# Window attention and a mixture of experts on one core: token repeats by DMA alone on two queues, the output sum on ScalarE and GpSimd, the selectors of the first norm later

## What is computed

```python
x = x + conv(_ln_c(x))        # norm over channels, then the attention layer
t = tokens(x)                 # 4096 tokens of 32 channels an image
t = t + ffn(_ln_t(t))         # norm over channels, then 8 experts, the best 2
# conv: instance norm over the picture with weight and bias; qkv = 1x1 conv;
#   windows of 8x8, 4 heads of 8 channels; softmax(q k / sqrt(8)) v; 1x1 projection
# ffn:  probs = softmax(x @ router_w + router_b); top 2, rescaled to sum 1;
#   y = sum over the two experts of p * (x @ expert_w[e] + expert_b[e])
```

## Time and profile before

| | us |
|---|---|
| runs | 397.84, 402.92, 404.67 |
| median | 402.92 |
| profiled execution | 405.62 |
| its span, first to last instruction | 403.6 |
| first scores (L596) start | 47.3 |
| last turn into the experts, about | 290 |

### The profile page before, as it was taken

One profiled execution on the slowest core, in us unless ns is written; L12 is line 12 of the kernel. 1 busy time (PEld: TensorE's weight loads), 2 busy tenths in 40 slices (PEclk: granted clock), 3 DMA queues, 4 the chain that ended last, 5 costly groups with the idle time before them and its releaser, 6 DMA issues.

```text
span 403.6 us, 12568 instructions
## 1 busy us (share of the span) xinstructions
PE 360.6 (89%) x5318; PEld 189.1 (47%) x5318; DVE 335.2 (83%) x435; ACT 260.5 (65%) x448; POOL 162.4 (40%) x191
## 2 busy tenths in 40 slices
PE   5979689999999999999999999998898897778985
PEld 2545446665665655566566656565421221111220
DVE  1477968988988979998998979999967999996785
ACT  3735557777787798678788797775464664423331
POOL 8600000111202202378634102478593558438543
PEclk9988969999999999999999999999998999896999
DMA  8600000031000000000000100022314543533541
GB/s 306 286 2 4 2 0 3 2 74 35 4 2 4 2 3 2 2 3 2 3 2 22 37 2 3 2 59 69 87 39 107 144 123 106 139 112 96 149 139 52
DMA packets 12870, 22.49 MB, mean 56 GB/s; under 512 B 2960, under 2 KB 5136, under 8 KB 12432
## 3 DMA queue, kind: packets, MB, share of 16 engines
q1 hardware_dynamic: 12240, 19.93, 17.1%
q10 hardware_dynamic: 576, 1.77, 1.1%
HBM read 5.96 MB, written 4.19 MB: 25 GB/s over the span
## 4 chain that ended last, share of the span: by engine, by line
PE 57%; DVE 24%; ACT 7%; issue 5%; DMA 4%; POOL 2%; ACTq 0%; POOLq 0%; DVEq 0%
PE psum L609 13%; PE psum L626 8%; PE psum L596 6%; PE psum L634 4%; PE psum L571 4%; DMA gate_f<-gate_sel 4%; PE psum L760 3%; PE psum L566 3%; PE psum L444 3%; DVE probs L1292 3%; DVE neg_max L1149 3%; DVE window_work L1152 2%; PE psum L772 2%; PE psum L580 2%; DVE probs L1289 2%
## 5 line engine op out<-in xcount | busy, mean ns | idle before, releaser
L327 POOL TENSOR_TENSOR o_norm<-o_tok,o_rden 128x128 f32<-128x128 f32 x64 | 25.4, 418 | 178.7 <-DVE o_rden L1162 178.7
L609 PE MATMUL psum<-weights_sb,window_work 128*128 128x128 f32 x512 | 82.1, 283 | 7.0 <-DVE window_work L1152 4.0
L894 ACT ACTIVATE probs<-psum 128x512 f32<-128x512 f32 x128 | 74.8, 595 | 17.5 <-PE psum L609 15.2
L609 PEld LDWEIGHTS psum<-weights_sb,window_work 128*128 128x128 f32 x512 | 57.9, 141 | 49.6 <-issue 28.8
L1152 DVE TENSOR_TENSOR window_work<-psum,neg_max 128x1024 f32<-128x1024 f32 x64 | 78.4, 1225 | 2.2
L1149 DVE TENSOR_REDUCE neg_max<-psum 128x16 f32<-128x1024 f32 x64 | 76.8, 1199 | 4.0 <-PE psum L596 4.0
L626 PE MATMUL psum<-probs,v_cols 128*32 128x64 f32 x2048 | 54.8, 225 | 0.3 <-DVE o_tok L1160 0.2
L626 PEld LDWEIGHTS psum<-probs,v_cols 128*32 128x32 f32 x2048 | 34.8, 109 | 28.2 <-issue 24.8
L878 ACT ACTIVATE stage<-k_sb,weights_sb 128x512 f32<-128x512 f32 x64 | 44.1, 719 | 0.0
L1160 DVE STREAM_TRANSPOSE o_tok<-psum 128x512 f32<-128x512 f32 x32 | 22.9, 716 | 21.1 <-PE psum L626 21.1
L596 PE MATMUL psum<-stage 32*64 32x256 f32 x1024 | 35.8, 387 | 1.9 <-DVE proj_bias L1136 1.0
(11 more groups left out here) (131 smaller groups left out, 612.4 us busy)
## 6 DMA issues: line engine op xcount, KB each, us to landing
stage<-act_all SPq DMA_DIRECT2D x144, 64.0 KB, 2.0
out<-out_sb SPq DMA_DIRECT2D x16, 256.0 KB, 2.0
stage<-in_x SPq DMA_DIRECT2D x3, 1024.0 KB, 12.4
gate_rows<-gate_parts SPq DMA_DIRECT2D x16, 128.0 KB, 2.6
weights_sb<-weights ACTq DMA_DIRECT2D x1, 811.5 KB, 11.7
stage<-in_x SPq DMA_DIRECT2D x1, 768.0 KB, 5.3
gate_f<-gate_sel ACTq DMA_DIRECT2D x1, 512.0 KB, 14.9
weights_sb<-weights ACTq DMA_DIRECT2D x1, 320.0 KB, 7.7
```

Source lines behind the costliest of these rows:

```text
L327: last = pool.tensor_tensor(o_norm[:, hf, :, p * 16:p * 16 + 16].rearrange("p g (b d) -> p g b d", b=2), t[:, p * 8:p * 8 + 8, :].rearrang ...
L609: last = nc.tensor.transpose(bank[TURN_BANKS[v % 2]][:, b * P:b * P + P], heads.rearrange("p h k -> p (h k)"), const["c_ident"][:, :])
L894: nc.scalar.activation(probs[:, w % 4, :], bank[TURN_BANKS[w % 2]][:, :], ACT.Exp).then_inc(exp_done, 1)
```

## The change

1. All four images of all chunks are repeated by DMA, two chunks in one (32 partitions by 4 KB). Slots hold a pair of chunks and there are three: `stage[:, 0:4096]`, `stage[:, 4096:8192]` and `x_win[:, 0:4096]`, which was the work space of the gates of quads 0 and 1. Pairs 0 and 1 are issued by SP alone; from pair 2 on SP issues images 2 and 3 and ScalarE's queue images 0 and 1, eight DMAs each. `replicate`, `keep_tokens` and `centre_rep` are gone. The queries move to `out_sb`.
2. The sum of a chunk: ScalarE copies the PSUM bank to `y_sb` (in the space of `v_cols`), GpSimd adds `act_all`. Only the last chunk is summed by VectorE. `bias` waits for the copy instead of the sum.
3. Gate step 21 of quads 2 and 3 moves from VectorE to GpSimd, and steps 22 and 23 stand together before the scaling of a half.
4. In the first norm the selector table is loaded ahead of the last piece of the weights, `regroup` is made first, and `sel_sum` between quads 0 and 1. `instance_deviation(1)` stands behind the forming of chunk 1's input, and TensorE waits for `biases_ready` only at the second turn of chunk 0.

```diff
-SPLITS, SLOTS = 3, 4
+SPLITS, SLOTS = 3, 3
...
-        q_two = stage[:, 0:2 * CHUNK].rearrange("p (u n) -> p u n", u=2)
-        x_rep = stage[:, :].rearrange("p (s b n) -> p s b n", s=SLOTS, b=IMG)
+        x_reps = [t.rearrange("p (b u n) -> p b u n", b=IMG, u=2)
+                  for t in (stage[:, 0:half], stage[:, half:2 * half], x_win[:, 0:half])]
+        q_two = out_sb
+        y_sb = v_flat[:, 0:2 * CHUNK].rearrange("p (u n) -> p u n", u=2)
...
+        def wait_tokens(engine, c):
+            pair = c // 2
+            k, turns = pair % SLOTS, pair // SLOTS
+            engine.wait_ge(reps_in[k], 16 * ((16 if k < REP_FIRST else 8) + 8 * turns))
+            by_act = 8 * turns + (0 if k < REP_FIRST else 8)
+            if by_act > 0:
+                engine.wait_ge(reps_by_act[k], 16 * by_act)
+        def repeat_pair(engine, pair, images, done):
+            at = slice(pair * 2 * CHUNK, (pair + 1) * 2 * CHUNK)
+            for b in images:
+                for e in range(4):
+                    engine.dma_start(x_reps[pair % SLOTS][C * e:C * e + C, b, :, :],
+                                     act_all[C * b:C * b + C, at].rearrange("p (u n) -> p u n", u=2)
+                                     ).then_inc(done[pair % SLOTS], 16)
+        def wait_slot(engine, pair):
+            if pair >= SLOTS:
+                engine.wait_ge(y_step, (pair - SLOTS) * 4 + 4)
+            elif pair == 2:
+                engine.wait_ge(gate_step[1], GATE_OPS + ONE)
+            elif pair == 1:
+                engine.wait_ge(score_ps, CHUNKS * 2)
...
-            for h, n in ((1, 6), (4, 14), (6, 22), (7, 23), (8, 26), (8, 27), (9, 29)):
+            for h, n in ((1, 6), (4, 14), (6, 21), (7, 22), (7, 23), (8, 26), (8, 27), (9, 29)):
...
# SP
+            def repeat_tokens(pair):
+                sp.wait_ge(x2_done, min(pair * 2 + 2, CHUNKS) + X2)
+                wait_slot(sp, pair)
+                repeat_pair(sp, pair, range(0 if pair < REP_FIRST else 2, IMG), reps_in)
...
             for c in range(CHUNKS):
-                if c + 3 < CHUNKS:
-                    repeat_tokens(c + 3)
                 if c % QUAD == 2 and c // QUAD + 1 < QUADS:
                     move_gates(c // QUAD + 1)
+                if c == 2:
+                    repeat_tokens(2)
+                if c >= 2 and c % 2 == 0 and c // 2 + 2 < CHUNKS // 2:
+                    repeat_tokens(c // 2 + 2)
...
# GpSimd, after scale(c, eh)
+                    if eh == 1 and c >= 1:
+                        combine(c - 1)
...
# TensorE
+                if n == 0 and v == 1:
+                    pe.wait_ge(biases_ready, 1)
...
-            pe.wait_ge(biases_ready, 1)
+            pe.wait_ge(ln1["normed"], CHUNKS + NORMED)
             chunk(0, 0, first=True)
...
-                wait_past(pe, summed, c - 1)
+                wait_past(pe, y_kept, c - 1)
...
# ScalarE
+            act.dma_start(gate_in, io["gate_sel"]).then_inc(gate_in_loaded, 16)
             act.dma_start(weights[:, second_cols:], io["weights"][:, second_cols:]).then_inc(weights_loaded, 16)
-            act.dma_start(gate_in, io["gate_sel"]).then_inc(gate_in_loaded, 16)
...
+                    if first and hf == 0:
+                        instance_deviation(1)
...
+            def keep_sum(c):
+                act.wait_ge(y_step, c * 2 + 2)
+                wait_past(act, summed, c - 1)
+                nc.scalar.activation(y_sb[:, c % 2, :], bank[6 + c % 2][:, :], ACT.Copy).then_inc(y_kept, 1)
...
                     copy_gates(c, eh)
+                    if eh == 1 and c >= 1:
+                        keep_sum(c - 1)
...
-                    if eh == 0 and c + REP_FIRST < CHUNKS:
-                        keep_tokens(c + REP_FIRST, 0)
+                    if (c, eh) == (2, 1):
+                        repeat_tokens(2)
+                    if eh == 0 and c >= 3 and c % 2 == 1 and (c + 3) // 2 < CHUNKS // 2:
+                        repeat_tokens((c + 3) // 2)
...
# VectorE
-            selectors()
+            regroups()
             for quad in range(QUADS):
+                if quad == 1:
+                    selectors()
                 first_norm(quad)
...
-            HALF_STEPS = ((0, 1, 2), (3, 4, 5), (7, 8), (9, 10, 11, 12), (13,), (15, 16), (17, 18, 19, 20, 21), (24,))
+            HALF_STEPS = ((0, 1, 2), (3, 4, 5), (7, 8), (9, 10, 11, 12), (13,), (15, 16), (17, 18, 19, 20), (24,))
...
-                    if eh == 0 and c >= 1:
-                        combine(c - 1)
```

More of the change, by code:

```diff
@@ L182, in metaformer_block @@
         reps_in = [sem(f"reps_in{k}") for k in range(SLOTS)]
-        rep_ps = sem("rep_ps")
-        rep_done = sem("rep_done")
+        reps_by_act = [sem(f"reps_by_act{k}") for k in range(SLOTS)]
         raw_done = sem("raw_done")
@@ L430, in _ @@
                     for quad, n in late:
-                        if n != 23:
+                        if n not in (22, 23):
                             gates(quad, n)
@@ L732, in _ @@
                 chunk(m, m % 2, final=(m == CHUNKS - 1))
-            def replicate(c, first_bank):
-                for b in range(2):
-                    rows = slice(32 * b, 32 * b + 32)
-                    last = nc.tensor.matmul(bank[first_bank + b][:, :], centre_rep[rows, :],
-                                            act_all[rows, c * CHUNK:c * CHUNK + CHUNK], start=True, stop=True)
-                last.then_inc(rep_ps, 1)
             def gate_pair(c, eh, pair):
@@ L1008, in copy_gates, with repeat_tokens @@
                 nc.scalar.activation(gate_copy[eh][:, :], bank[2][:, :], ACT.Copy).then_inc(gate_copied, 1)
[L1010 to L1016 removed]
+            def repeat_tokens(pair):
+                wait_slot(act, pair)
+                repeat_pair(act, pair, range(2), reps_by_act)
+            def keep_sum(c):
+                act.wait_ge(y_step, c * 2 + 2)
+                wait_past(act, summed, c - 1)
+                nc.scalar.activation(y_sb[:, c % 2, :], bank[6 + c % 2][:, :], ACT.Copy).then_inc(y_kept, 1)
             exps(CHUNKS - 1, NW - 2)
@@ L1265, in combine @@
                 dve.wait_ge(y_step, c * 2 + 2)
[L1266 removed]
+                dve.wait_ge(summed, c)
+                dve.wait_ge(stored[c % 2], c // 2 * 16)
                 nc.vector.tensor_tensor(
```

92 lines of the change are left out of this document (28 added, 64 removed).

## The result

The changed kernel takes 406.9 us in the median of 15 runs (403.46 to 409.79), the kernel before, run on the same chips, 403.62 (397.84 to 405.62). The ratio is 1.012, with a 95% interval of 1.007 to 1.017: within 2%, but slower, where 390.7 and 3.0% faster was forecast. The profiled execution of the changed kernel (403.46) was the fastest of its runs and had a granted clock of 0.962; the run at the median had 0.944. The profiled one of before (405.62) was its slowest.

The account below looks back on a forecast made before the run. TensorE was taken to bound attention; in the expert stage VectorE, later TensorE and VectorE in turns. Front 8.2 plus stage 4.0 gave 12.2 us: 393.4 for the profiled execution, 390.7 from the median, 3.0% less; range 384 to 402.

Parts of the forecast that it names:

- The front: First norm and first attention chunk, before the expert stage: 8.2 us gained, 5.5 plus 2.7.
- the selectors: First norm: selectors later and table loaded earlier start quad 0's norm at 17.9 instead of 21.46; gain 5.5 us.
- the first chunk: First attention chunk: earlier chunk 1 input lets VectorE go on at 55.9 instead of 58.65; gain 2.7 us.
- a pair costs ScalarE one block of 8 x 0.62 = 5.0 us: Expert stage: ScalarE's eight repeat issues per pair hold its gate copy; uncovered only at chunk 11, costing 2.0 us.
- rival 1: Expert stage: ScalarE's issues are dearer and it becomes the bound; break-even 1.26 us an issue, 420 at 1.7; chance 0.11.
- 7.3 us of the engines in 9.5 to 15 us: Expert stage: a pair's 2.1 MB of repeats takes the DMA engines 7.3 us at 289 GB/s.
- GpSimd's sum 1 ends 308.7, and SP, which stores it, moves the gates of quad 1 and only then issues pair 2.: Expert stage, chunk 2: SP reaches pair 2 at 311.9, landed 319; chunk 4 starts at 318.9, 2.2 us ahead.
- 0.4 later than before, twice: Late gates: with step 21 on GpSimd, its three products in a row end 0.4 us later, for two quads.
- Clock: Expert stage: GpSimd is the later engine around chunk 10, so a drop of TensorE's clock costs 0.6 to 1 us.
- Rival 2: Expert stage: GpSimd or the lower clock eats its gain, leaving only the front's 8.2 us: 394.7; chance 0.24.
- the stage's gain: Expert stage: 4.0 us gained, taken from an end 4.5 us ahead less the cost of a clock drop.
- four such meetings: Chunks 5 to 9: GpSimd's third operation a chunk makes VectorE wait at the port four times more, 0.3 to 1.2 us each.

Follow-up runs that it names:

- experiment 1: The kernel before with part 4 of the change alone (load order, selectors, deviation, bias wait): 395.58 us, ratio 0.985.
- Experiment 5: The changed kernel with ScalarE's eight repeat issues spread, two behind each half's copy (pair 2: four and four): 399.93 us, ratio 0.995.
- experiment 4: The changed kernel with the sum and gate step 21 back on VectorE: 401.62 us, ratio 0.994.
- experiment 14: The changed kernel with the sum and gate step 21 back on VectorE and ScalarE's repeat issues spread: 398.72 us, ratio 0.988.
- Experiment 3: The kernel before with part 4 and the sum on ScalarE and GpSimd, replication still by TensorE: 406.52 us, ratio 1.007.
- experiment 7: The kernel before with part 4 and the sum on ScalarE and GpSimd, plus SP's store one chunk later in its queue: 395.62 us, ratio 0.983.
- experiment 10: The changed kernel with only the store one chunk later in SP's queue: 401.06 us, ratio 0.992.
- experiment 15: The changed kernel with ScalarE's repeat issues spread and gate step 21 back on VectorE: 398.47 us, ratio 0.986.
- experiment 11: The changed kernel without ScalarE's repeats (images 0 and 1 of chunks 4 to 15), so not computing everything: 393.78 us, ratio 0.978.
- experiment 6: The changed kernel with all repeats issued by SP, none by ScalarE: 403.89 us, ratio 1.001.
- experiment 9: The changed kernel with ScalarE's issues spread, each store one chunk later, and quad 1's gates and SP's pair 2 repeats one chunk earlier: 402.97 us, ratio 0.997.

## Why the prediction was wrong

**Right.**
- The front, 8.2 us: measured 9.2 in the trace and 8.5 by experiment 1. Its two terms are less exact than their sum: the selectors, forecast 5.5, gave 5.1, and the first chunk, forecast 2.7, about 4. The quad norms start at 18.23, 25.26 and 32.18 (forecast 17.9, about 25.3, 32.6), the second half's first scores at 50.22 (forecast 50.4). From 21.5 to 41 us TensorE's clock was 1.00 and not 0.82, as the working said: it no longer stood idle before it spread quad 1.
- The middle DMA issue, 0.62 us, and the sum on GpSimd, 1.27 at best (its mean is 1.40, in part beside VectorE).
- The period at the end, forecast 4.74 and measured 4.75. The chain of the changed kernel, GpSimd's products of the last chunks:

```profile
386.24 1.27 POOL probs L422
...
390.99 1.27 POOL probs L422
...
395.74 1.27 POOL probs L422
```

**Wrong, step by step.**
1. *"a pair costs ScalarE one block of 8 x 0.62 = 5.0 us"*, covered everywhere but at chunk 11. The blocks are 5.3 to 7.6 us, and 6.06 at chunk 11. The price of an issue was the middle one of a time when SP's queue had the engines for itself; with two queues on full engines single issues go up to 1.5 us on ScalarE and 2.0 on SP (up to 2.1 before too, where it stood on SP alone). And the cover was counted to within a few tenths of a microsecond, so a block 1 to 2.5 us longer than forecast could come through. Experiment 5 puts the blocks at 7.0 us in this kernel, against 2.0 forecast; with the sum on VectorE they are worth 2.9 (experiments 4 and 14). The mechanism was there, in the forecast and in rival 1, and chunk 11 was the right place for most of it; the size was wrong. The rival itself, with a break-even at 1.26 us an issue, didn't happen: the middle issue stayed at 0.62.
2. *"7.3 us of the engines in 9.5 to 15 us"* and, for the landing, *"2.6 is taken"*. The capacity of 289 GB/s was an average over a queue that moved large blocks from outside too. The stretch with the engines full moved 256 GB/s, and the bytes came in a lump: pairs 2 and 3 and the gates of quad 1 within 20 us. SP reached the gates of quad 1 when the forecast had it there (300.13; forecast 308.7 less the front's 8.2), but they took 4.19 us to issue instead of 2.55, the repeats behind them 6.16 instead of 4.9, and the last one 4.54 to land. The forecast let chunk 4 wait 1 us; it waited 5.4.
3. *"GpSimd's sum 1 ends 308.7, and SP, which stores it, moves the gates of quad 1 and only then issues pair 2."* The order was read rightly for chunk 2 and then dropped: in chunks 3 to 15 no step asks what stands in SP's queue behind a store whose sum now ends half a chunk later. Experiment 3 against 7 gives the price where it stands alone, 10.9 us; experiment 10 gives it in the changed kernel, 5.8. SP's move of the gates of quad 3, due at chunk 12, doesn't occur in the schedule at all.
4. *"0.4 later than before, twice"* for step 21: two delays of 0.4 less two products of 0.61 would be a gain of 0.4. The waits grew by 2.0, from 1.6 to 3.6, and experiment 15 makes the move a loss of 1.5.
5. *Clock.* The forecast had a drop cost at most 1 us. With TensorE waiting for copies, gates and repeats, it was 0.70 in one stretch of 10 us and 0.78 to 0.88 in most of the stage. Experts and bias at 1.94 and 2.08 in chunk 11's turn alone are 2.0 us. In experiment 11, where the waits are gone, the stretch from 310 to 320 runs at 1.00. The lower clock stands here where the waits are, and makes the matmuls behind them dearer; how much of the loss is its own, no run separates.

Rival 2 named GpSimd and port meetings as what would eat the stage's gain. The forecast counted four such meetings more than before. There are none more: three of VectorE's gate steps took over 1.25 us in the changed kernel's stage (1.26 to 1.83, where 0.68 to 0.70 is the undisturbed time), and three in the kernel before (1.32, 1.33 and 1.58). And experiment 7 leaves no net price for GpSimd's 15 sums. The result, 406.9, lies outside the range of 384 to 402: among the cases only rival 1 let the stage lose more than the front gave.

The Trainium skill says in its first page, Trainium Kernel Development and Optimization, section Key Constraints, that DMAs issued from several engines run on the same 16 DMA engines, and that issuing from several at once only saves the issue time. By that the second queue should have been worth at most SP's issue time and no bandwidth. The rows agree on the bandwidth: 256 GB/s (300 to 310 us) and 236 (experiment 5, 310 to 320 us) at a DMA share of 1.00 with two queues, and 227 at 0.91 with SP alone (experiment 6, 350 to 360 us), from which I estimate 249 for full engines. On the time they go further: in blocks on ScalarE the second queue costs (406.9 against 403.9 with all on SP), spread out it gains (399.9).

**Open.** How the loss divides between ScalarE's block and the full engines: experiment 11 takes both away, experiment 5 only the first, and the contributions overlap. Whether an order of SP's queue exists in which repeats by DMA beat TensorE's: experiments 9 and 14 each ran into the next wait, and a third place in `out_sb` wasn't tried. And the two profiles of the changed kernel are of its shortest run and of a long one, so how a run at the median shares out its further 3.4 us was not seen directly.

## What to carry to other kernels

When an operation moves to another engine and ends later, write down every in-order queue that waits for it, the DMA queue of SP first of all, and what stands behind that wait: here the operation had no net cost and the queue behind its store cost 10.9 us. Count DMA bytes in the burst in which they are issued, not over the stage, and issue them in ones and twos between an engine's own work, not in blocks. Leave room for the opposite case too: a store behind a long row of issues held up the output buffer in experiments 6 and 9. The best complete kernel of this study is the smallest edit: part 4 alone, 395.6 us, 1.5% [0.7%, 2.4%] less than before by the ratio; experiment 7 is level with it.

## What the runs showed of the hardware

- With the DMA share at 1.00 the engines moved 256 GB/s in the changed kernel and 236 in experiment 5 (310 to 320 us), nearly all of it 128 KB copies inside SBUF, below the 289 that the average of queue q1 gave.
- The time to issue a DMA isn't fixed: gate moves that took 0.603 to 0.642 us before took up to 1.66 when two queues fed full engines, and their landing went from 2.6 to 4.5 in the middle.
- A ScalarE queue that issues DMAs holds its compute instructions for the whole block: its compute side stood idle for 7.08 us beside 7.55 us of issues.
